# Biased cross-attention on one core: VectorE adds the bias to the newest scores first, and subtracts the maximum from the block four ahead between the two halves of the running maximum

## The reference, cut to what matters

```python
def _L1_xattn_ref(queries, keys, values, attn_bias, Wq, Wk, Wv, Wp):
    q = _split_heads(queries @ Wq.T, 16, 64)
    k = _split_heads(keys @ Wk.T, 16, 64)
    v = _split_heads(values @ Wv.T, 16, 64)
    scores = jnp.einsum('bhqd,bhkd->bhqk', q, k) * 256 ** (-0.5) + attn_bias
    weights = jax.nn.softmax(scores, axis=-1)
    out = jnp.einsum('bhqk,bhkd->bhqd', weights, v)
    return out.transpose(0, 2, 1, 3).reshape(2, 256, 1024) @ Wp.T
```

## Time and profile before

| | us |
|---|---|
| median of 3 runs | 2041.51 (2040.83 to 2046.22) |
| the profiled execution, its own time | 2046.66 |
| its span in the profile | 2044.9 |
| busy over the span: TensorE | 1871.3 (92%) |
| busy: VectorE | 1637.4 (80%) |
| busy: GpSimd | 926.0 (45%) |
| busy: ScalarE | 839.7 (41%) |

### The profile page before, as it was taken

The page is one execution under the profiler, slowest core; times in us unless marked ns, Lnnn a source line. Parts: engine busy times, 40 slices in busy tenths (PEclk is TensorE's granted clock), DMA queues, the critical chain, the costliest instruction groups (busy, mean ns, idle before and its releaser), DMA issues. The chain is left out here.

```text
span 2044.9 us, 42828 instructions
## 1 busy us (share of the span) xinstructions
PE 1871.3 (92%) x16712; PEld 1270.3 (62%) x16714; DVE 1637.4 (80%) x2124; ACT 839.7 (41%) x1119; POOL 926.0 (45%) x434
## 2 busy tenths in 40 slices
PE   7999999999778969989999999999999999998737
PEld 4566666666437858866665666666666666656425
DVE  4666767668886445689999999999999999999873
ACT  3666656566430124414333343334433343333401
POOL 0356645466450014206554665547555665546300
PEclk9999999999988669999999999999999999999857
DMA  3000210000030032100000000020000000000100
GB/s 131 9 14 0 74 33 13 9 3 9 24 117 1 1 127 79 46 13 7 13 13 12 1 13 13 13 82 13 13 13 13 0 13 13 13 8 1 47 1 11
DMA packets 27742, 52.59 MB, mean 26 GB/s; under 512 B 4243, under 2 KB 15268, under 8 KB 27172
## 3 DMA queue, kind: packets, MB, share of 16 engines
q1 hardware_dynamic: 27216, 51.60, 7.6%
q10 hardware_dynamic: 468, 0.16, 0.0%
HBM read 51.23 MB, written 0.52 MB: 25 GB/s over the span
## 5 line engine op out<-in xcount | busy, mean ns | idle before, releaser
L345 POOL TENSOR_TENSOR biased_sums<-biased_sums,biased_scores 128x1024 f32<-128x1024 f32 x216 | 513.6, 2378 | 151.4 <-ACT biased_scores L621 135.2
L682 DVE TENSOR_TENSOR biased_scores<-ps,bias 128x1024 f32<-128x1024 f32 x256 | 313.2, 1224 | 34.8 <-PE ps L421 29.8
L696 DVE TENSOR_TENSOR ps<-ps,biased_scores 128x512 f32<-128x512 f32 x480 | 336.6, 701 | 4.1
L703 DVE TENSOR_TENSOR biased_scores<-biased_scores,ps 128x1024 f32<-128x1024 f32 x256 | 307.2, 1220 | 1.3 <-PE ps L472 1.3
L345 POOL TENSOR_TENSOR plain_sums<-plain_sums,plain_scores 128x1024 f32<-128x1024 f32 x104 | 247.7, 2381 | 66.5 <-ACT plain_scores L621 57.4
L421 PE MATMUL ps<-biased_queries,keys_again 64*128 64x256 f32 x2048 | 261.1, 391 | 13.7 <-DVE biased_scores L682 12.8
L621 ACT ACTIVATE biased_scores<-biased_scores 128x1024 f32<-128x1024 f32 x256 | 258.8, 1051 | 20.4 <-DVE biased_scores L703 19.4
L379 PE MATMUL ps<-weights_again,context_again 128*64 128x128 f32 x4096 | 249.5, 275 | 2.8 <-ACT biased_values L605 1.4
L379 PEld LDWEIGHTS ps<-weights_again,context_again 128*64 128x64 f32 x4096 | 225.1, 137 | 40.7 <-issue 19.1
L433 PE MATMUL ps<-biased_scores,biased_values 128*64 128x256 f32 x2048 | 244.3, 380 | 1.0 <-ACT biased_scores L621 0.7
L368 PE MATMUL ps<-context_again,weights_again 128*64 128x512 f32 x960 | 231.8, 603 | 13.1 <-ACT keys_again L594 10.5
(11 more groups left out here) (392 smaller groups left out, 2330.4 us busy)
## 6 DMA issues: line engine op xcount, KB each, us to landing
context<-in_ctx_t SPq DMA_DIRECT2D x8, 1024.0 KB, 5.4
context_again<-in_ctx_t SPq DMA_DIRECT2D x8, 1024.0 KB, 7.4
moe_w<-in_moe_w SPq DMA_DIRECT2D x32, 256.0 KB, 2.8
weights_again<-in_wqkv SPq DMA_DIRECT2D x45, 128.0 KB, 2.2
bias<-in_fside SPq DMA_DIRECT2D x1, 4096.0 KB, 15.0
biased_w_out<-in_w_out SPq DMA_DIRECT2D x16, 256.0 KB, 2.6
weights<-in_wqkv SPq DMA_DIRECT2D x21, 128.0 KB, 2.2
plain_w_out<-in_w_out SPq DMA_DIRECT2D x8, 256.0 KB, 2.6
```

Source lines behind the costliest of these rows:

```text
L345: pool.tensor_tensor(both(SUM[:, :, :, :]), both((E[:, 0] if kp == 1 else SUM)[:, :, :, :]), both(E[:, kp, :, :, :]), ALU.add).then_inc(su ...
L682: dve.tensor_tensor(E[:, kp, :, :, :].rearrange("p (h t) n j -> p h t (n j)", h=2), scores_bank(kp).rearrange("p (h t n) -> p h t n", h=2, ...
L696: ins = dve.tensor_tensor(to, highest, E[:, kp, :, n, :], ALU.max)
L703: dve.tensor_tensor(at, at, c.ps[:, LOWER, :].rearrange("p (a j) -> p a j", a=HQ).unsqueeze(2) .to_broadcast([P, HQ, 2, P]), ALU.add).then ...
```

## The change

In the biased stage a step of VectorE had the order lower (four ahead), first half of the maximum, bias, second half. It becomes bias, first half, lower (four ahead), second half. The plain stage keeps its order, as does everything on the other engines.

```diff
                 def sweep(m, attending, scoring):
                     for kp in range(NP):
+                        if scoring and biased:
+                            scores_out(m + 1, kp, attending)
+                        if scoring and kp > 0:
+                            peak(m + 1, kp - 1, 0)
                         if biased and attending and kp + AHEAD < NP:
                             lower(m, kp + AHEAD)
-                        if scoring and kp > 0:
-                            peak(m + 1, kp - 1, 0)
-                        if scoring and biased:
-                            scores_out(m + 1, kp, attending)
-                            if kp > 0:
-                                peak(m + 1, kp - 1, 1)
+                        if scoring and biased and kp > 0:
+                            peak(m + 1, kp - 1, 1)
```

## The result

The changed kernel takes 2071.72 us (median of 4 runs, 2068.48 to 2074.91) against 2041.17 for the kernel before (median of 4, 2040.04 to 2046.22). The ratio is 1.0145 with a 95% interval of 1.0121 to 1.0169: slower by 30.5 us. The forecast was 2067.4, or 25.9 slower than the 2041.51 known then, in a range of 2056 to 2075.

A forecast was written before the change was run, and what follows sets the result against it. VectorE's and TensorE's chains to `turn_peaks`, equal within 0.17 us, were taken to bound it. 1.13 + 0.10 + 0.65 - 0.17 = 1.71 us in 14 sweeps, plus 0.73 and 1.2, made 25.9 slower: 2067.4 us, range 2056 to 2075.

The forecast's parts named there:

- slack of 0.17: End of a sweep: VectorE is 0.17 us ahead of TensorE at `turn_peaks`; any larger VectorE loss lengthens the sweep.
- (a): Head of each sweep: the `lower` of block 4 leaves VectorE's idle hole and adds 1.13 us to its busy chain.
- (b): `scores_out` comes earlier in its step and may find no scores: a wait of 0.10 us before `scores_out(4)`.
- (c): Later exponentials delay ScalarE's copies: K0 loses 0.30 us, VectorE waits 0.65 before `scores_out(6)`; K2's delay is covered.
- (d): Halves of the maximum: nothing in the 15 sweeps, 0.73 us more in the first sweep, behind its last wait.
- (e): GpSimd's sums cost nothing; in sweep START, GpSimd releases `scores_out(0)` and the same 1.13 us applies.
- (f): Sweeps END-2 and END-1: END-2 costs 1.2 us with no slack to take off; END-1 keeps the old order.
- Rival 1: Scores(6) are in time, so only the moved `lower` of block 4 counts: 0.96 us per sweep, 2057 us; chance 0.13.
- Rival 2: ScalarE holds V2, V3 and V5, so TensorE ends last: 0.7 us more per sweep, 2077 us; chance 0.07.
- Rival 3: Faster: TensorE's wait of 0.41 us at 1099.21 goes and TensorE sets the period, 2035.8 us; chance 0.04.
- Rival 4: No measurable change: waits only move, and slack in later steps takes back the loss at the head; chance 0.05.
- Rival 5: TensorE's clock falls because it idles more often: 1.04 us per sweep, 15.6 on top, 2083 us; chance 0.02.

The follow-up runs named there:

- v5_first: Changed kernel, with ScalarE copying piece V5 ahead of the exponential of block 13 instead of behind it: period 66.91 us, 2069.93 us in one run.
- late4: Kernel before, with only the `lower` of block 4 moved behind `scores_out(0)`: period 66.08 us, 2062.03 us in one run.
- new_hoist4: Changed kernel, with the `lower` of block 4 put back ahead of `scores_out(0)`: period 66.73 us, 2069.31 us in one run.
- v2_first: Changed kernel, with ScalarE copying piece V2 ahead of the exponential of block 7 instead of behind it: period 66.52 us, 2069.12 us in one run.
- ahead5: Kernel before, with VectorE lowering five blocks ahead, blocks 4 and 5 before `scores_out(0)`: period 64.28 us, 2034.84 us against 2041.93, ratio 0.9963.

## Why the prediction was right, and where its sizes were off

**The bound.** That the chain from `scores_out(0)` to the last half of the maximum sets the period was right for the changed kernel: TensorE waits for that half at `turn_peaks`, and v5_first takes 1.47 us of waiting from TensorE and leaves the period at 66.91. The slack of 0.17 was a little too large. At the start of `turn_peaks` it was there (0.92 behind the last half before, 0.74 now), but `turn_peaks` itself takes 0.07 longer when it had to wait. `find_peaks` waited 0.86 for it before and 0.75 now; the difference of 0.11 is the slack that counts. A second link escaped me. In the kernel before, the chain that sets the period does not run to the last half: TensorE's wait at scores(13) hangs on `scores_out(11)`, so there a delay of VectorE is passed on in full with no slack to take off. late4 shows it: 1.13 more, and not 0.96, with no wait at `turn_peaks`. I saw it only before late4, and used it in its expectation.

**(a), the `lower` in the hole.** Confirmed by size alone (late4: 1.13). But as a share of this change's loss it was given too much. new_hoist4 gives back 0.18. The sum of (a), (b) and (c) came out nearly right because the three terms are one account: with (a) removed, the waits of (b) grow. The simpler account uses one fixed point. `scores_out(6)` stands where TensorE's scores(6) allow it, 0.35 us later than before against `scores_out(0)`: the 0.39 of K0, less 0.04, for before the change scores(6) were ready only 0.04 us ahead of VectorE. Behind it VectorE has 31.47 us to the last half (1148.27 to 1179.74), where it had 29.74 (1080.64 to 1110.38). The difference of 1.73 is half a step: the `lower` and a half of the maximum that the change moved from ahead of that wait to behind it. 1.73 + 0.35 - 0.11 = 1.97, and 1.96 was measured. Without K0's delay it gives 1.58, and v2_first measured 1.57.

**(b) and (c), the new waits.** Both came at the places named. Sizes: 0.19 and not 0.10 before `scores_out(4)` (12.84 us behind `scores_out(0)`, where 12.65 was wanted), because the scores are ready after 1.27 and not 1.18; 0.74 and not 0.65 before `scores_out(6)` (20.50, where 12.84 + 6.92 = 19.76 was wanted), because the wait at K0 costs 0.39 and not 0.30. With the slack these make 1.13 + 0.19 + 0.74 - 0.11 = 1.95 where the prediction has 1.71, and 0.24 over 14 sweeps is 3.4 of the 4.7 us by which the forecast fell short of the growth of the stage. The rest is the 1.7 of the clock in one sweep, 0.3 in END-2, 0.4 and 0.3 the other way in the first sweep and behind the last `find_peaks`. That the total came within 5 us is helped by these terms partly cancelling, and the 1.7 was in no term. K2 was late by 1.41 and covered, as said; v5_first shows that the cover held.

**(d), the first sweep.** It cost 0.32 and not 0.73. The extra half is there (`x3` and one more behind the last `scores_out`), but the five steps before it are shorter: from `scores_out(10)` to `scores_out(15)` it takes 12.32 (896.30 to 908.62), and it took 12.68 (900.24 to 912.92). Two halves of one block behind each other take 1.42, while the second half of one block and the first of the next took 1.49 in that sweep, though only 1.43 in the steady ones. Why is open.

**(e)** held: no new wait for GpSimd. In sweep START its release of `scores_out(0)` is waited for 6.18 us and not 5.06, with the `lower` of block 4 gone from in front of it.

**(f), END-2** cost 1.53 and not 1.2. TensorE's clock fell once there, behind a wait of 1.95 for VectorE (8 matmuls in 2.08 us and not 1.13):

```profile
1891.95 2.08 PE L421 MATMUL ps<-biased_queries,keys_again 64*128 64x256 f32 x8 [1.95 <-DVE biased_scores L682]
```

That falls at a point where VectorE is the later engine, and the trace of v5_first, where VectorE has the same order, separates it. There the same wait of 1.95 is followed by matmuls at full clock:

```profile
1889.84 1.14 PE L421 MATMUL ps<-biased_queries,keys_again 64*128 64x256 f32 x8 [1.95 <-DVE biased_scores L686]
```

Its sweep END-2 takes 66.17 and not 66.37. So up to 0.2 us go with the clock, and 1.33 are left, which is 1.13 + 0.20 as (f) has it, with the larger wait of (b).

**The rivals.** Rival 1 (only (a) counts) has its own kernel in late4: a period of 66.08, less than the 66.91 measured. Rival 2 (ScalarE holds TensorE so long that it ends last) fell by v5_first; V3 did not make TensorE wait. Rival 3 (faster) fell with the slack: the wait at scores(13) did go away, which was a gap on the busiest engine, and the kernel got slower. Rival 4 (no change that can be measured) fell by the total: the ratio's interval starts at 1.0121. "Perfetto Trace Analysis" of the Trainium skill, section Optimization Strategy, is no wrong advice here, but incomplete: it names the gap and what blocks it, and not what is queued behind the instruction that is pulled forward. ahead5 follows the same rule and gains. Rival 5 (the clock) was seen at two places of the stage where the trace of before has none, worth 1.7 us at the first and up to 0.2 at the second, and in no steady sweep.

## What to carry to other kernels

In an in-order queue, ask of each moved instruction whether it now stands ahead of or behind the next wait that it can't shorten: what was done while waiting for another engine is free, and the same work behind that wait costs its whole length, as the 1.13 us of late4 did. Find the last such wait of a period and count what the engine still has to do behind it; gains ahead of it are lost again in the wait. And when two engines are within 0.2 us of each other, look for a place to put work into the idle hole, as ahead5 does, before bringing a wait's release forward.

## What the runs showed of the hardware that I had not expected

- The idle that the profile shows at a wait of TensorE is less than the wait costs. Start to start, an idle of 0.41 at scores(13) cost 0.67 us per sweep (64.95 against 64.28 in ahead5), 0.32 at K0 cost 0.39, and 0.55 at `turn_peaks` cost 0.71 (1178.80 to 1180.48 is 1.68, where 0.97 is usual). With no wait, the record of one group of matmuls ends after the next has started (1.13 long and the next after 0.97, 2.00 long and the next after 1.93), and the idle is counted from that end; 0.16 + 0.55 = 0.71 and 0.07 + 0.32 = 0.39. The ends of matmuls are modelled in the profile. A group of scores can also be held inside its record with no idle shown at all, as by 0.40 us in g = 7 of v5_first.
- After an almost equal wait for a transfer, 2.62 and 2.66 us, TensorE went on at full clock in one trace and at the lower one in another, for 1.7 us of difference. In the eleven traces of this case the clock stayed after waits of 2.54, 2.54, 2.57 and 2.62 us and fell after 2.56, 2.62, 2.62, 2.66, 2.76, 2.83 and 3.00, so between 2.56 and 2.62 us the length of the wait doesn't tell.
- The time from the start of TensorE's scores to the VectorE instruction that they release was 1.18 us behind a piece in the first sweep and 1.27 in the others, and an added wait of VectorE that is already met did not change the 1.18.
